# Where GpSimd waits for its scatters, in a gated attention and mixture-of-experts kernel on one core

## The reference, cut to what matters

```python
# x, ctx: [32, 128, 128] f32; 16 heads of 8; 8 experts, top 2, F = 512
def reference(x, ctx, mask, g_xattn, g_ffn, wq, ..., gate_w, w1, w3, w2):
    x = x + tanh(g_xattn[0]) * attention(layernorm(x), ctx, mask)     # windowed, 16 global tokens, softmax
    x = x + tanh(g_ffn[0])   * experts(layernorm(x))
    return x

def experts(x):
    probs = softmax(x @ gate_w)                    # [b, t, 8]
    weights, chosen = top_k(probs, 2); weights = weights / weights.sum(-1)
    out = 0
    for i in range(8):
        wi = where(chosen == i, weights, 0).sum(-1)
        out = out + (silu(x @ w1[i]) * (x @ w3[i])) @ w2[i] * wi[..., None]
    return out
```

## Time and profile before

| | us |
|---|---|
| Median of three runs (lowest, highest) | 478.28 (475.81, 478.28) |
| The profiled execution: its own time | 475.07 |
| its span, first to last instruction | 473.4 |
| Busy: PE / DVE / ACT / POOL | 415.8 / 296.3 / 238.4 / 262.4 |
| Mean granted TensorE clock, share of full speed | 0.961 |

### The profile page before, as it was taken

One profiled execution on the slowest core, in us unless ns is written; L12 is line 12 of the kernel. 1 busy time (PEld: TensorE's weight loads), 2 busy tenths in 40 slices (PEclk: granted clock), 3 DMA queues, 4 the chain that ended last, 5 costly groups with the idle time before them and its releaser, 6 DMA issues.

```text
span 473.4 us, 14424 instructions
## 1 busy us (share of the span) xinstructions
PE 415.8 (88%) x4555; PEld 365.8 (77%) x4556; DVE 296.3 (63%) x807; ACT 238.4 (50%) x564; POOL 262.4 (55%) x322
## 2 busy tenths in 40 slices
PE   2879979999888888797888899989999999999990
PEld 1656758877666666575666799989999999999990
DVE  4957788897666667687765466785554554455530
ACT  3848425666555566474665454434444444444430
POOL 5955445234535453535464677885656565666552
PEclk9979979999999999898998899999999999999996
DMA  8965456467576667549212323334443343334221
GB/s 218 266 116 86 110 105 171 90 96 141 138 121 116 129 98 128 131 79 269 81 52 68 86 41 52 57 64 75 69 52 49 50 50 53 49 54 56 25 27 12
DMA packets 74847, 44.14 MB, mean 93 GB/s; under 512 B 8704, under 2 KB 71586, under 8 KB 74658
## 3 DMA queue, kind: packets, MB, share of 16 engines
q1 hardware_dynamic: 59040, 33.79, 33.9%
q0 software_dynamic: 12400, 8.92, 13.8%
q10 hardware_dynamic: 3360, 0.83, 1.0%
HBM read 16.02 MB, written 12.10 MB: 59 GB/s over the span
## 4 chain that ended last, share of the span: by engine, by line
PE 68%; DVE 9%; ACT 7%; issue 6%; another core or an unknown queue 5%; DMA 2%; ACTq 1%; POOL 0%; DVEq 0%; POOLq 0%
PE ps_scores L1786 26%; PE ps_max_scores L1794 13%; PE ps_values L943 6%; PE ps_max_scores L896 5%; PE ps_scores L926 4%; PE ps_max_scores L880 3%; ACT pT L1081 2%; DVE rsplit L1185 2%; PE ps_scores L880 2%; PE ps_values L1777 2%; PE ps_out L961 2%; DVE qkf L589 2%; PE ps_out L967 1%; DMA bk_col<-in_L_xattn_bk_dram 1%
## 5 line engine op out<-in xcount | busy, mean ns | idle before, releaser
L1910 POOL DMA_INDIRECT out_dram<-va,xg x71 | 115.8, 1631 | 63.1 <-issue 28.1
L1786 PE MATMUL ps_scores<-xgT,qs 128*128 128x128 f32 x1136 | 141.6, 279 | 2.7 <-issue 2.3
L1786 PEld LDWEIGHTS ps_scores<-xgT,qs 128*128 128x128 f32 x1136 | 134.8, 195 | 3.7 <-issue 2.8
L1185 DVE TENSOR_REDUCE rsplit<-ps_max_scores 128x4 f32<-128x512 f32 x128 | 85.0, 685 | 32.5 <-PE ps_max_scores L880 18.0
L1872 DVE TENSOR_TENSOR qs<-qs,ps_scores 128x512 f32<-128x512 f32 x71 | 48.8, 687 | 80.3 <-PE ps_scores L1786 58.1
L1424 POOL DMA_INDIRECT expert_rows_scratch<-xr,pos x64 | 65.9, 1030 | 48.3 <-ACT pT L1081 22.5
L1794 PE MATMUL ps_max_scores<-w_all,qs 128*128 x568 | 75.8, 277 | 1.6 <-DVE qs L1872 1.0
L1081 ACT ACTIVATE pT<-ps_scores 128x1024 f32<-128x1024 f32 x64 | 62.5, 1022 | 25.3 <-PE ps_scores L880 12.9
L1794 PEld LDWEIGHTS ps_max_scores<-w_all,qs 128*128 128x128 f32 x568 | 69.5, 193 | 2.4 <-issue 2.4
L1834 ACT ACTIVATE qs<-ps_scores 128x512 f32<-128x512 f32 x71 | 42.3, 596 | 36.3 <-PE ps_scores L1786 29.3
L1741 DVE COPY qs<-w_all 128x1024 f32 x71 | 50.9, 717 | 9.6 <-issue 3.7
(11 more groups left out here) (239 smaller groups left out, 547.4 us busy)
## 6 DMA issues: line engine op xcount, KB each, us to landing
qs<-w_all SPq DMA_DIRECT2D x96, 64.0 KB
ks<-w_all SPq DMA_DIRECT2D x96, 64.0 KB
w_all<-in_L_ffn_w_dram SPq DMA_DIRECT2D x24, 256.0 KB
xg<-expert_rows_scratch SPq DMA_DIRECT2D x71, 65.0 KB
xs<-in_x_dram SPq DMA_DIRECT2D x4, 512.0 KB, 5.7
out_dram<-xs SPq DMA_DIRECT2D x8, 256.0 KB
out_dram<-va,xg POOLq DMA_INDIRECT x71
expert_rows_scratch<-fill SPq DMA_DIRECT2D x16, 65.0 KB
```

The source lines that it names most:

```text
L1185: nc.vector.tensor_reduce(rsplit[:, at.c % 2, 0, n * HB:(n + 1) * HB], ps1[:, n % 2].rearrange("p (h s) -> p h s", h=HB), AX.X, ALU.max).t ...
L1786: ins = nc.tensor.matmul(bank[u % 2][:, c * P:(c + 1) * P], w13[:, u % 2, n, c * P:(c + 1) * P], xgT[:], start=True, stop=True)
L1910: pool.indirect_dma_start(out=out_rows, out_offset=bass.IndirectOffsetOnAxis(ap=xg_u[:, u, X_IDX:X_IDX + 1], axis=0), in_=yt[:, u], in_off ...
```

## The change

Three things are changed. First, GpSimd's attention step: the wait for the landing after a group's eighth scatter is gone; the first scatter of a step now stands ahead of the deviations, and the deviations of group r (from the second on) wait for the landing of group r-2's scatters. So that this wait has a positive value in every case, a fifth small first send is counted on `scattered[1]`, and all waits on that semaphore are raised by 16. Second, empty tiles: their row numbers begin at 128 in place of 0, and `order_rest` computes the entry of the last run in two added instructions, 1 only where the last expert's last tile can hold rows of the first two groups. Third, the block is opened with `no_gpsimd_drain=True`.

```diff
-            pool.iota(first_rows[:], [[P, SENDS]], base=0, channel_multiplier=1).then_inc(first_ready, 1)
-            def empty_send(u):
+            pool.iota(first_rows[:], [[P, SENDS + 1]], base=0, channel_multiplier=1).then_inc(first_ready, 1)
+            def empty_send(u, landed):
...
                 if g < SENDS:
-                    empty_send(g)
+                    empty_send(g, sent[g])
+                elif g == SENDS:
+                    empty_send(g, scattered[1])
...
-                pool.iota(fill_u[:, E:2 * E, X_IDX], [[P, E]], base=0, channel_multiplier=1).then_inc(fill_ready, 1)
+                pool.iota(fill_u[:, E:2 * E, X_IDX], [[P, E]], base=P, channel_multiplier=1).then_inc(fill_ready, 1)
...
-                if (r := route(at, 2)):
-                    route_std(r)
-                    route_tokens(r)
                 if at.known and at.b == 2:
                     padding_rows()
                 if sent.exists():
                     if at.j == 0:
                         place_rows(sent)
                     scatter(sent, range(2 * at.j, 2 * at.j + 1))
+                if (r := route(at, 2)):
+                    if r.is_past(1):
+                        pool.wait_ge(scattered[r.u], r.half * (2 * GB * 16) + 16 * r.u)
+                        stand_alone(pool)
+                    route_std(r)
+                    route_tokens(r)
+                if sent.exists():
                     pool.wait_ge(exp_done, at.b * 2 + 2)
                     stand_alone(pool)
                     scatter(sent, range(2 * at.j + 1, 2 * at.j + 2))
-                if at.j == 3 and sent.exists() and (not at.known or sent.g + 2 < NG):
-                    pool.wait_ge(scattered[sent.u], sent.half * (2 * GB * 16) + 2 * GB * 16)
-                    stand_alone(pool)
...
             def route_last():
+                pool.wait_ge(scattered[LAST.u], LAST.half * (2 * GB * 16) + 16 * LAST.u)
                 route_std(LAST)
...
+            end = bump[:, 2 * E - 1:2 * E]
+            plan_then(dve, nc.vector.scalar_tensor_tensor(out=end, in0=nt_f[:, E - 1:E], scalar=float(P),
+                                                          in1=cnt[:, 2 * E - 1:2 * E], op0=ALU.mult, op1=ALU.subtract))
+            plan_then(dve, nc.vector.tensor_scalar(end, end, float(P), None, ALU.is_lt))
...
-                sp.wait_ge(scattered[u], NG // 2 * (2 * GB * 16))
+                sp.wait_ge(scattered[u], NG // 2 * (2 * GB * 16) + 16 * u)
...
-                sp.wait_ge(scattered[u], len(range(u, EARLY, 2)) * (2 * GB * 16))
+                sp.wait_ge(scattered[u], len(range(u, EARLY, 2)) * (2 * GB * 16) + 16 * u)
...
-        with nc.Block() as block:
+        with nc.Block(no_gpsimd_drain=True) as block:
```

More of the change, by code:

```diff
@@ L85, in build @@
     rows_d = nc.dram_tensor("expert_rows_scratch", (E * CAP + E * P, XW), F32, kind="Internal").ap()
-    first_d = nc.dram_tensor("first_sends_scratch", (SENDS * P, 1), F32, kind="Internal").ap()
+    first_d = nc.dram_tensor("first_sends_scratch", ((SENDS + 1) * P, 1), F32, kind="Internal").ap()
     out_rows = out.rearrange("b s d -> (b s) d")
@@ L435, in project_gpsimd @@
                 pool.iota(t, pattern, base=base, channel_multiplier=mult, allow_small_or_imprecise_dtypes=True)
-            pool.iota(first_rows[:], [[P, SENDS]], base=0, channel_multiplier=1).then_inc(first_ready, 1)
-            def empty_send(u):
+            pool.iota(first_rows[:], [[P, SENDS + 1]], base=0, channel_multiplier=1).then_inc(first_ready, 1)
+            def empty_send(u, landed):
                 pool.indirect_dma_start(
                     out=first_d, out_offset=bass.IndirectOffsetOnAxis(ap=first_rows[:, u:u + 1], axis=0),
-                    in_=ident[:, u:u + 1], in_offset=None).then_inc(sent[u], 16)
+                    in_=ident[:, u:u + 1], in_offset=None).then_inc(landed, 16)
             pool.wait_ge(first_ready, 1)
@@ L1514, in build @@
         token_b = sb("token_b", [P, 2], BF16)[:, 0:1]
-        first_rows = sb("first_rows", [P, SENDS], U32)
+        first_rows = sb("first_rows", [P, SENDS + 1], U32)
         lifted = sb("lifted", [P, 1])
```

## The result

| | before | after |
|---|---|---|
| Median, us (lowest, highest; runs) | 478.28 (475.81, 479.56; 4) | 460.12 (456.2, 464.26; 4) |
| Ratio, 95% interval | 1 | 0.960 (0.952 to 0.968) |
| Profiled execution: its own time, span | 475.07, 473.4 | 456.2, 454.1 |

The median of all four, 460.12, lies just inside it; the ratio leaves out one slower execution, of 464.26. By the profiled executions the change gives -18.9.

The account below looks back on a forecast made before the run. The chain runs over TensorE for 68% of the span; attention groups with scatters leave it some 4 to 6 us unfilled. Terms -5.3 - 1.3 + 0.4 - 5.5 = -11.7 take 478.28 to 466.6 us, range 459.5 to 473.5.

Parts of the forecast that it names:

- The drain, -5.3: Block's exit: without GpSimd's DRAIN of 5467 ns after the last landing, the kernel ends 5.3 us earlier.
- Empty tiles, -1.3: Kernel's end: send 69 no longer waits for send 68's landing, so the last send ends 1.29 us earlier.
- `order_rest`, +0.4: Two added VectorE instructions on the chain, 0.20 us each, all paid because TensorE waits: 0.40 us longer.
- the fifth first send, 0: GpSimd's added first send, 1044 ns, falls into an idle gap of about 2 us and costs nothing.
- Attention, -5.5: Batches with scatters: moving the landing wait gives -6.0 us, moving the deviations costs +0.5.
- Its first part: First two batches of the loop's four groups: a later first scatter saves 1.5 us per group, -6.0.
- The second part: Third batch, where the first scatter moves ahead of the deviations: +0.1 us in each of five groups, +0.5.
- Rival 2: Attention gives twice as much, -12 us, because third and fourth batches gain as well: 460.1 us; chance 0.13.
- Rival 1: Attention gives nothing, since scatters take their share of TensorE wherever they stand: 472.1 us; chance 0.30.
- The rule weighed against the trace: Attention: engine and DMA ports are disjoint, so the scatters' place would be indifferent and attention's term 0.
- Rival 4: Attention: deviations behind a scatter come late beyond the 0.6 us slack, so the kernel is slower, 481.2 us; chance 0.05.

Follow-up runs that it names:

- experiment 1: Kernel before with only GpSimd's drain at the block's exit removed, on a 449 us chip: 442.92 against 448.85 us, ratio 0.989.
- experiment 13: Kernel before with only GpSimd's drain at the block's exit removed, on a 475 us chip: 470.18 us, ratio 0.988.
- 5: Kernel after with the deviations ahead of the third batch's first scatter again, on a 449 us chip: 444.05 us, ratio 0.988.
- experiment 9: Kernel after, unchanged, run again on a 475 us chip: 455.72 against 475.46 us, ratio 0.960.
- experiment 12: Kernel after with the deviations ahead of the first scatter again, landing wait still moved, on a 475 us chip: 468.60 us, ratio 0.983.
- experiment 2: Kernel before with only the empty-tiles change and its two instructions in order_rest, on a 449 us chip: 448.37 us, ratio 1.000.
- 4: Kernel after with the landing wait at a group's end put back, on a 449 us chip: 443.41 us, ratio 0.989.
- 11: Kernel after with the landing wait at a group's end put back, on a 475 us chip: 465.09 us, ratio 0.976.
- experiment 3: Kernel after with GpSimd's drain and the old empty tiles, so only the scatter part changed, on a 449 us chip: 448.97 us, ratio 1.001.
- 8: Kernel before, unchanged, run again on a 475 us chip: 476.81 us, ratio 1.002.
- experiment 10: Kernel after with GpSimd's drain and the old empty tiles, so only the scatter part changed, on a 475 us chip: 462.12 us, ratio 0.972.
- experiment 6: Kernel after with two more indirect DMAs per batch in batches 0 to 7, 128 rows of one number each: 461.63 us, one execution.

## Why the prediction was wrong, point by point

- **The drain, -5.3: right.** -5.1 on a 449 us chip (experiment 1), -5.7 on a 475 us chip (experiment 13). Outside the span the kernel after has 2.1 us in place of 1.7, so at most 0.4 comes back.
- **Empty tiles, -1.3: mis-sized.** The row moved by 0.94: the wait for the landing of send t-1 is gone, but send 69 starts 1.12 after its result and not 0.78. It does so in experiments 5, 9 and 12 too, but starts after 0.78 or 0.79 in 2, 4 and 11. The profile names send 68's landing as the releaser, but that comes 0.01 after the start (445.57 + 3.03), so it is hardly the cause; the 0.34 stay open. With the old table the start comes 2.06 to 3.76 after the result (before, 1, 3, 8, 10, 13), so the row of one trace was also a poor measure of the wait.
- **`order_rest`, +0.4, and the fifth first send, 0: right.** 0.39 by the rows, and 0.34 between tiles 17 and 18 on a 449 us chip (4.44 in experiment 2, 4.10 in 1). The first exponential of attention starts at 69.4 in place of 69.2, and at 68.4 in experiment 9.
- **Attention, -5.5: the term that failed.** Measured between the first exponentials of batches 8 and 31: 139.6 to 127.1 in the first pair of traces, -12.5, and -13.2 by experiment 10's ratio. Its first part was right: the first two batches of the four groups of the loop went from 51.7 to 44.9, -6.8 against -6.0. The second part was not: "I take +0.1 in each of five groups: +0.5" for the batches with the deviations. They went from 63.2 to 56.5, -6.7. With the old order put back (experiment 12) they take 65.0. There I looked at when GpSimd's instructions end, and not at which of TensorE's products end beside the scatters and are seen late, although the same row that carried the first part, a gap of TensorE's reader beside two scatters, stands in just these batches. The sum also stopped at batch 31: from there to tile 0, where three scatters stand behind the last deviations (247.22, 248.64 and 250.14 in before), another 2.8 us went. It is 11.9 to 12.6 us with the old order (before, 8, 12, 13) and 9.3 to 9.9 with the new one (after, 9, 10, 11). And it had no term for the clock, though the earlier trace rows showed 0.93 in the loop's last group; how much of the -12.5 the clock gives back was not told apart.
- **Rival 2, -12, given 0.13**, is what happened, for its stated reason: the third and fourth batches gain as well. **Rival 1**, attention gives nothing, is what happens on the 449 us chips (experiment 3). The two are one change on two kinds of chip, which the profile of one chip could not tell. That the measured time met rival 2's 460.1 so closely is in part luck: in the traces attention gave -12.5 and -2.8, and 2.6 were lost at tiles 10 to 17.
- **The rule weighed against the trace.** The Trainium skill, "SBUF — State Buffer", section "SBUF: two separate sides", would make the scatters' place indifferent. On the 449 us chips experiment 3 agrees (1.001); on the 475 us chips experiment 10 does not (0.972). The records point to the message that a product is finished, not to the product itself: TensorE's next matmuls run on while the reader waits. But the ends of TensorE's instructions are modelled in the profile, so that the product itself is late is not excluded.
- **Rival 4.** Its sign shows once: ScalarE waits 0.88 us for GpSimd's `shift` before `norm_rows` at 234.2, and batch 30 takes 4.68 us in place of 3.91 (4.70 in experiment 9, 4.69 in 10). Elsewhere the slack held.

What is shown: GpSimd's indirect DMAs make TensorE's messages late, up to 4.1 us on the 475 us chips and nearly always under 1.5 on the others; moving the wait and the deviations takes the lateness from 124 to 84 us and brings 13 us there; and the order alone carries the gain of the third and fourth batches. That closeness of the scatters is what counts is argued from the traces of 9, 11 and 12 and was not shown. What makes a chip one kind or the other stays open.

## What to carry to other kernels

When a reader of TensorE waits for nothing that the profile can name, look at GpSimd's indirect DMAs in the same microsecond, and price each place where a product ends beside one of them, not only the one with the named wait. A wait on an engine off the chain can matter by what it pushes together afterwards. Before pricing such a term, measure the kernel before on more than one chip: here the scatter part is worth 2.8% on one kind (experiment 10) and nothing on the other (experiment 3).

## What the runs showed of the hardware that was not expected

- The same program takes about 475 or 449 us, some 6% apart. Most of the difference lies in batches with scatters (batches 8 to 31: 139.6 us in the trace of before, 117.8 in experiment 1, which lacks only the drain at the end) and none in those without (39.1 in both).
- Messages of TensorE's finished products come late beside GpSimd's indirect DMAs, by up to 4.09 us; those of the other three engines do not (0.01 us).
- "Remote" waits for TensorE's products, 1 to 4 us each, sum to 26 to 43 us between 108 and 230 us in the traces of the two unchanged kernels on the first chip, and to 0 to 2.2 us on the 449 us chips, experiment 6 apart; the messages there are late too, by 10 to 21 us in all, but nearly all by less than the 1.5 us from which the word is used.
- GpSimd's DRAIN at the block's exit takes 5467 ns behind indirect DMAs, to the nanosecond the same in every trace that has it, and 172 to 176 ns at the program's start.
